# A two-block MLP kernel on one core: one padded round trip through DRAM per tile, and a re-ordered switch between its two phases

## What is computed

```python
# block 0
agg_w, agg_b = per_batch_mix(att(cond_128))          # att: softmax over 8 experts
h0   = einsum('boi,bih->boh', agg_w, x) + agg_b      # mixes the 64 rows of each batch
main = h0 @ weight.T                                 # 1024 x 1024
w    = top-2 gate of h0, with a capacity count over all 4096 rows
lora = sum_e (w_e * (h0 @ lora_A[e])) @ lora_B[e] / 16
x1   = x + main + lora
# block 1
c1   = grouped_conv1d(x1, 64 -> 64 channels, 4 groups, 9 taps) + ctx + bias
res  = c1 @ W.T + b
w1   = softmax_e(<c1 Wq_e, c1 Wk_e>)
out  = x1 + res + sum_e w1_e * (c1 @ A[e]) @ Bm[e]
```

## Time and profile before

| | |
|---|---|
| median of three runs | 1290.04 us (1289.51 to 1290.76) |
| the profiled execution | 1290.04 us |
| its span on the core | 1288.3 us |
| PE busy | 1279.4 us of the span |
| granted TensorE clock | 1.00 over the span |
| DVE, ACT, POOL busy | 714.7, 280.4, 239.1 us |
| DMA | 141.55 MB, mean 110 GB/s |

### The profile page before, as it was taken

How to read it: one execution, slowest core, us unless ns; L and a number is a source line. 1 busy time by engine, 2 the same in 40 slices (tenths; PEclk the granted TensorE clock), 3 DMA queues, 4 the chain that set the end, 5 groups by cost and what they waited for, 6 DMA issues and landing times.

```text
span 1288.3 us, 20752 instructions
## 1 busy us (share of the span) xinstructions
PE 1279.4 (99%) x7223; PEld 1193.6 (93%) x7223; DVE 714.7 (55%) x1727; ACT 280.4 (22%) x515; POOL 239.1 (19%) x173
## 2 busy tenths in 40 slices
PE   9999999999999999999999999999999999999998
PEld 8999999999999998989889889988988988988997
DVE  6887877767777776634434444444443444344432
ACT  6323322222322234211111111111111111111110
POOL 2344522232322330001001001001100100100100
PEclk9999999999999999999999999999999999999999
DMA  8245433333333357434223323322422322342310
GB/s 292 91 133 182 147 114 109 120 128 114 118 109 112 104 195 236 121 88 119 72 71 115 91 69 104 104 69 88 119 70 84 113 80 69 106 102 70 91 47 33
DMA packets 83735, 141.55 MB, mean 110 GB/s; under 512 B 6641, under 2 KB 52081, under 8 KB 83697
## 3 DMA queue, kind: packets, MB, share of 16 engines
q1 hardware_dynamic: 83696, 141.06, 36.1%
HBM read 88.59 MB, written 52.45 MB: 109 GB/s over the span
## 4 chain that ended last, share of the span: by engine, by line
PE 92%; DVE 4%; DMA 1%; issue 1%; POOL 0%; ACT 0%; SPq 0%; DVEq 0%; POOLq 0%; ACTq 0%
PE ps L1205 28%; PE ps L1207 27%; PE ps L1206 27%; PE ps L1346 6%; PE ps L1347 2%; DMA staging<-in_w 1%; DMA z<-in_cpack 0%; DVE weights L877 0%; DVE row L910 0%; POOL mixw L581 0%; DVE part L902 0%; DVE mix_hl L887 0%; PE ps L1439 0%; DVE mixs L884 0%; PE ps L1322 0%
## 5 line engine op out<-in xcount | busy, mean ns | idle before, releaser
L1205 PE MATMUL ps<-weights,lhs_h 128*128 128x512 f32 (+2 forms) x1408 | 498.4, 354 | 0.8 <-issue 0.8
L1207 PE MATMUL ps<-weights,lhs_l 128*128 128x512 f32 (+2 forms) x1408 | 490.2, 348 | 0.0
L1206 PE MATMUL ps<-weights,lhs_h 128*128 128x512 f32 (+2 forms) x1408 | 489.1, 347 | 0.0
L1205 PEld LDWEIGHTS ps<-weights,lhs_h 128*128 128x128 f32 x1408 | 264.8, 188 | 23.9 <-issue 1.1
L1207 PEld LDWEIGHTS ps<-weights,lhs_l 128*128 128x128 f32 x1408 | 264.3, 188 | 20.8
L1206 PEld LDWEIGHTS ps<-weights,lhs_h 128*128 128x128 f32 x1408 | 264.7, 188 | 20.1
L645 POOL TENSOR_TENSOR xo<-row,wsum 128x512 f32<-128x512 f32 x60 | 76.8, 1306 | 662.4 <-DMA out_x<-xo 662.4
L1205 PE MATMUL ps<-weights 128*128 128x396 f32 x384 | 133.0, 346 | 0.0
L1206 PE MATMUL ps<-weights 128*128 128x396 f32 x384 | 132.3, 344 | 0.0
L1207 PE MATMUL ps<-weights 128*128 128x396 f32 x384 | 132.2, 344 | 0.0
L1177 DVE TENSOR_TENSOR xo<-ps,xo 128x512 f32<-128x512 f32 x64 | 43.1, 691 | 148.3 <-PE ps L1207 148.2
(11 more groups left out here) (151 smaller groups left out, 1436.0 us busy)
## 6 DMA issues: line engine op xcount, KB each, us to landing
row<-spill SPq DMA_DIRECT2D x30, 576.0 KB, 4.3
xo<-in_xt SPq DMA_DIRECT2D x32, 512.0 KB, 3.8
z<-x_round SPq DMA_DIRECT2D x64, 256.0 KB, 5.3
out_x<-xo SPq DMA_DIRECT2D x31, 512.0 KB, 2.7
x_round<-row SPq DMA_DIRECT2D x60, 256.0 KB, 2.0
row<-in_xr SPq DMA_DIRECT2D x31, 394.0 KB, 3.2
spill<-row SPq DMA_DIRECT2D x31, 394.0 KB, 4.0
staging<-in_w SPq DMA_DIRECT2D x8, 832.0 KB, 6.6
```

The lines of the kernel that those rows point to most:

```text
L1205: pe.matmul(out_ap, lhs[0], rhs[0], start=first, stop=False, skip_group_check=True)
L1206: pe.matmul(out_ap, lhs[0], rhs[1], start=False, stop=False, skip_group_check=True)
L1207: return pe.matmul(out_ap, lhs[1], rhs[0], start=False, stop=last, skip_group_check=True)
```

## The change

It has five parts.

1. x1_round is laid out as rows of 129 elements, one for each batch and position group, with the zero column in place. Each store writes four pieces of 512 B per partition instead of one of 2 KB; one z_load reads whole rows of 516 B on all 128 partitions instead of two that read 512 B on 64 partitions. Both stores of a buffer count on one semaphore, and z_load waits once. The order of positions on the partitions, and with it the convolution's weights, is laid out anew.
2. The POOL memset of z moves from tile 2 to tile 6, and at the end of tile 6 SP waits for it and writes z to both buffers of x1_round (padded); the first x1_store waits for these two.
3. The four chunks split aside move from tiles 4 to 7 to tiles 1 to 4. N1+4 is now split by POOL in the first tile of phase B, not by DVE.
4. At tile 24, DVE's x_low goes ahead of the second route; before, it came after the next y_low and evict.
5. At the switch the orders of SP, ACT, DVE and PE change: loads of N1+3, N1+5 and N1+6 go out earlier, z_high(0) and z_low(0) come after the splits of N1+3, N1+6 is split ahead of gates(2) and of z(1), and PE has no second(0,0,2,0,4) between n=5 and n=6 any more (it comes after conv(1,0), as in the other tiles).

```diff
-        x1_round = nc.dram_tensor("x1_round", (2, 2, P, D // 2), F32, kind="Internal").ap()
+        x1_round = nc.dram_tensor("x1_round", (2, BG, GC * S, W), F32, kind="Internal").ap()
+        def half_rows(u, h):
+            return x1_round[u].rearrange("b (c s) w -> (b c) s w", s=S)[:, S // 2 * h:S // 2 * h + S // 2, :]
...
-        by_pool = (N_LB0, N_CONV, N_LB1, N1)
+        by_pool = (N_LB0, N_CONV, N_LB1, N1, N1 + 4)
-        aside = {4: N_LB0, 5: N_CONV, 6: N_LB1, 7: N1}
+        aside = {1: N_LB0, 2: N_CONV, 3: N_LB1, 4: N1}
...
-                    sp.dma_start(x1_round[u, h], src[:, q]).then_inc(x1_out[h], 16)
+                    sp.dma_start(half_rows(u, h)[:, :, w:w + P],
+                                 src[:, 512 * h:512 * h + 512].rearrange("p (s i) -> p s i", i=P)
+                                 ).then_inc(x1_out[u], 16)
...
-                for h in range(2):
-                    sp.wait_ge(x1_out[h], out_done)
-                    sp.sem_inc(passed_sp, 1)
-                    w = 1 - h
-                    sp.dma_start(z[64 * h:64 * h + 64, :, w:w + P], positions(u, h)).then_inc(z_in, 16)
+                sp.dma_start(z[:, :, :], x1_round[u].rearrange("b q w -> q b w")).then_inc(z_in, 16)
...
+                if at(t, 6):
+                    sp.wait_ge(blank, 1)
+                    for k in range(2):
+                        sp.dma_start(x1_round[k].rearrange("b q w -> q b w"), z[:, :, :]).then_inc(padded, 16)
...
-            z_load(0, 0)
             chunk(N1 + 3)
+            z_load(0, 0, 0)
             chunk(N1 + 4)
+            x1_store(1, 1)
             sp.wait_ge(mix_read[2], TILES - 2)
             spill12(TILES - 3, 1)
-            x1_store(1, 1)
+            chunk(N1 + 5)
             sp.wait_ge(mix_read[2], TILES - 1)
             spill12(TILES - 2, 0)
-            chunk(N1 + 5)
-            z_load(1, 1)
+            z_load(1, 1, 0)
+            chunk(N1 + 6)
...
-                if at(t, 2):
+                if at(t, 6):
                     pool.memset(z[:, :, :], 0.0).then_inc(blank, 1)
...
+                if at(t, 0):
+                    split_lo(N1 + 4)
...
+            split_hi(N1 + 3)
+            y_high(TILES - 2, 2)
             z_high(0)
-            y_high(TILES - 2, 2)
-            split_hi(N1 + 3)
             split_hi(N1 + 4)
             conv_high(0, 0)
             y_high(TILES - 1, 2)
             split_hi(N1 + 5)
+            split_hi(N1 + 6)
             z_high(1)
-            split_hi(N1 + 6)
...
-                    if at(t, CATCH_UP + 1):
-                        y_low(t + 2, 0)
-                        evict(t - 1, 1 - u, 2)
-                        x_low(t + XB - 1, (b + XB - 1) % XB)
-                    else:
-                        evict(t - 1, 1 - u, 2)
-                        y_low(t + 2, 0)
+                    evict(t - 1, 1 - u, 2)
+                    y_low(t + 2, 0)
...
+                    if before_end(t, XB):
+                        x_low(t + XB, b)
                     if at(t, CATCH_UP):
                         route(t + 2, u)
-                    elif before_end(t, XB):
-                        x_low(t + XB, b)
...
             y_low(T1, 2)
+            x1_add(1, 1)
+            evict(T1, 1, 2)
+            split_lo(N1 + 3)
+            y_low(T2, 2)
             z_low(0)
-            y_low(T2, 2)
-            evict(T1, 1, 2)
-            x1_add(1, 1)
-            split_lo(N1 + 3)
             evict(T2, 0, 2)
             conv_read_low(0, 0, 0)
             y_low(T3, 2)
-            split_lo(N1 + 4)
             evict(T3, 1, 2)
             split_lo(N1 + 5)
+            split_lo(N1 + 6)
             gates(2, 0, 1)
...
-            main(T3, B3, 2, 0, 2)
+            main(T3, B3, 2, 0, 3)
+            mix(T2, B2, 2)
             pe.wait_ge(*low_of(N_CONV))
             conv(0, 0)
-            mix(T2, B2, 2)
             conv(0, 1)
-            main(T3, B3, 2, 2, 8)
+            main(T3, B3, 2, 3, 8)
...
-                        if n == 6:
-                            second(0, 0, 2, 0, 4)
```

More of the change, by code:

```diff
@@ L86, in program @@
         cond_rows = nc.dram_tensor("cond_rows", (B, C), F32, kind="Internal").ap()
-        x1_round = nc.dram_tensor("x1_round", (2, 2, P, D // 2), F32, kind="Internal").ap()
+        x1_round = nc.dram_tensor("x1_round", (2, BG, GC * S, W), F32, kind="Internal").ap()
         def f32(ap):
             return ap.bitcast(F32)
-        def positions(u, h):
-            return x1_round[u, h].rearrange("(b c) (s i) -> (c s) b i", c=GC, i=P)
+        def half_rows(u, h):
+            return x1_round[u].rearrange("b (c s) w -> (b c) s w", s=S)[:, S // 2 * h:S // 2 * h + S // 2, :]
         weights = sb("weights", [P, J * OUT1 * 2], F32R)
@@ L224, in program @@
         x1_out, z_in = pair("x1_out"), sem("z_in")
-        blank = sem("blank")
+        blank, padded = sem("blank"), sem("padded")
         z_hi, z_lo = sem("z_hi"), sem("z_lo")
@@ L432, in x1_store @@
                 src = x1_row(t, u)
+                if at(t, 0):
+                    sp.wait_ge(padded, 32)
                 if later(t, 2):
-                    loaded_before, = counts(t * 32 - 32)
+                    loaded_before, = counts(t * 16 - 16)
                     sp.wait_ge(z_in, loaded_before)
@@ L438, in x1_store, with z_load @@
                     sp.wait_ge(x1_ready, ready[h])
-                    q = slice(512 * h, 512 * h + 512)
-                    sp.dma_start(x1_round[u, h], src[:, q]).then_inc(x1_out[h], 16)
[L442 to L445, removed]
+                    w = 1 - h
+                    sp.dma_start(half_rows(u, h)[:, :, w:w + P],
+                                 src[:, 512 * h:512 * h + 512].rearrange("p (s i) -> p s i", i=P)
+                                 ).then_inc(x1_out[u], 16)
+            def z_load(t, u, it):
+                out_done, split_before = counts((it + 1) * 32, t * 2)
+                sp.wait_ge(x1_out[u], out_done)
                 if later(t, 1):
@@ L448, in z_load @@
                     sp.wait_ge(z_lo, split_before)
-                    sp.sem_inc(passed_sp, 1)
-                for h in range(2):
-                    sp.wait_ge(x1_out[h], out_done)
-                    sp.sem_inc(passed_sp, 1)
-                    w = 1 - h
-                    sp.dma_start(z[64 * h:64 * h + 64, :, w:w + P], positions(u, h)).then_inc(z_in, 16)
+                sp.sem_inc(passed_sp, 1)
+                sp.dma_start(z[:, :, :], x1_round[u].rearrange("b q w -> q b w")).then_inc(z_in, 16)
             def phase_a(t, b, it):
@@ L522, in _ @@
             spill12(TILES - 1, 1)
-            chunk(N1 + 6)
             chunk(N1 + 7)
@@ L526, in _, with next_row @@
             sp.wait_ge(spilled0[1], TILES // 2 * 16)
-            def next_row(t, u):
-                added, left = counts(t * 2 - 2, t * 16 - 16)
+            def next_row(t, u, it):
+                added, left = counts(t * 2 - 2, it * 32)
                 sp.wait_ge(xb_ready, added)
-                for h in range(2):
-                    sp.wait_ge(x1_out[h], left)
-                    sp.sem_inc(passed_sp, 1)
+                sp.wait_ge(x1_out[u], left)
+                sp.sem_inc(passed_sp, 1)
                 load_row(t, u)
@@ L547, in phase_b @@
                 if before_end(t, 3):
-                    next_row(t + 3, 1 - u)
+                    next_row(t + 3, 1 - u, it + u + 1)
                 if before_end(t, 2):
-                    z_load(t + 2, u)
+                    z_load(t + 2, u, it + 1)
                 if at(t, TILES - 1):
@@ L786, in z_high @@
                     if h == 0:
-                        act.wait_ge(z_in, t * 32 + 32)
+                        act.wait_ge(z_in, t * 16 + 16)
                         if later(t, 2):
@@ L1073, in conv_read_low @@
                 if at(t, 0):
-                    for k in range(2):
-                        dve.wait_ge(x1_out[k], 16)
+                    dve.wait_ge(x1_out[0], 32)
                     dve.wait_ge(xb_ready, 2)
@@ L1183, in phase_b @@
                     z_low(1)
-                    split_lo(N1 + 6)
                     split_lo(N1 + 7)
@@ L1433, in phase_b @@
                     pe.wait_ge(y_read, t * 2)
-                    second(t, u, 2, 0, 4)
+                second(t, u, 2, 0, 4)
                 if nxt:
@@ L1501, in laid_out @@
                     band[:, s, m, :, r, :] = w[:, :, :, tap].transpose(2, 0, 1)
-    a["conv"] = band.reshape(GC, 2, S // 2, -1).transpose(1, 0, 2, 3).reshape(P, 2 * GRP * P)
+    a["conv"] = band.reshape(P, 2 * GRP * P)
     return {k: np.ascontiguousarray(w) for k, w in a.items()}
```

## The result

| kernel | median us (range, runs) | before beside it | ratio, 95% interval |
|---|---|---|---|
| changed | 1299.53 (1296.63 to 1301.11, 4) | 1290.22 | 1.0069 [1.0051, 1.0089] |
| changed, a second time | 1299.03 (1296.95 to 1300.45, 4) | 1290.52 | 1.0068 [1.0052, 1.0084] |

A forecast was written before the change was run, and what follows sets the result against it. PE, busy 1279.4 of 1288.3 us, was taken as the bound. Terms 2.4 (tile 2) + 0 + 1.2 (tile 24) + 0.4 (switch) + 0 gave +4.0 on 1290.04: 1294.0 us, 8-in-10 range 1289.8 to 1298.

The forecast's parts named there:

- the term for z(0) in part 5: At the switch, z arrives at about 489, just in time for conv(0,0): 0.3 us, bounds 0 and 2.5.
- a sign of being wrong: In phase B, the stores landing beyond 6 us after issue would show the prediction wrong.
- The term beside it: At the switch, POOL's next add can hold gates(2) for one half, 1.3 us; taken as 0.5 us.
- The 2 us that the prediction gave this rule: In phase B, pieces not starting at 256 B multiples shift z by about 2 us, inside the cover; cost 0.
- Tile 2: POOL's early split holds DVE's line 890 until 73.6, fully exposed on PE: +2.4 us, bounds 0 and 2.8.
- The zeros: Writing zeros at tile 6's end makes later row loads some 5 us late: 0, up to 2 us if pieces are slow.
- Tile 24: x_low and evict ahead of y_low(27,0) add 1.6 us, less hold by POOL's add: +1.2 us, bounds 0.8 to 1.6.
- The switch's orders: At the switch, old gaps close but PE waits 1.7 us at tw_turn(2): -0.4 us before the added terms.
- Phase B: In the rest of phase B, later z is covered by idle time: cost 0, period of 24.6 us unchanged.
- Rival B: Small pieces are slow: conv(0,0) waits 2.5 us at the switch, zeros cost 2; +8, 1298 us; chance 0.12.

## Why the prediction was wrong

**The step that failed** is the term for z(0) in part 5: "a store to 512 B pieces lands between 2.0 us (the 2 KB stores now) and 5.3 us (the loads of 512 B pieces) after its issue ... I take 0.3 for it, bounds 0 and 2.5". Its upper bound came from loads. The stores took 7.1 and 10.5 us at the switch, beyond the 6 us that the prediction itself had named as a sign of being wrong, and z came at 497.3 instead of 489. The runs with aligned pieces show why: for the most part it is where a stored piece begins.

The step also looked only at z. The stores slow the transfers that share the queue with them, and SP stands behind them with the loads of N1+4 and then N1+6. That chain ended at tw_turn(2), and the slow load of N1+3 at mix(T2,2). By the ratios the whole change costs 4.1 us with aligned stores and 8.8 with these: the term of 0.3 was about 4.6 (2 to 7), its bound of 2.5 most likely too low. The term beside it, 0.5 for POOL's add holding gates(2), measured 1.1 in this profile (1.35 us instead of 0.29) and 0 in the second, where gates(2) began 0.09 us before POOL's add.

The prediction weighed a page's rule on pieces that don't start at a multiple of 256 B (the Trainium skill, DMA: Bandwidth & Descriptors, section How a descriptor splits into AXI transactions). It speaks of what a transaction can read; here the loads of 516 B pieces did not suffer, and the stores did. The 2 us that the prediction gave this rule, hidden in phase B, were worked out from no row, and it did not ask what the rule would do at the switch.

**The clock was not in the sum.** After gaps of 2 to 3 us PE ran at 1.2 GHz for some microseconds: 1.6 us lost behind tile 2, 1.6 in conv(0) and 1.4 behind tw_turn(2) in the first profile (from the spacing of the matmuls), 1.5 in all in the second. Over all runs of the changed kernel the granted clock was 0.996 to 0.999, of the kernel before 0.999 or 1.

**Tile 2: the mechanism right, the size too small.** Line 890, now 895, was predicted to last 2.8 us and lasted 3.33; PE was to wait until about 82.0 and waited until 82.24. The gaps grew by 3.0 us in the first profile, 2.4 or 2.5 in the second and with the splits alone, against +2.4. But with the small gaps of tiles 3 and 5 the splits alone cost 3.5 us, and in the first profile the lower clock came on top. The Trainium skill's rule on the port pair (SBUF — State Buffer, section SBUF: two separate sides) is borne out once more: 0.47 us became 2.60 to 3.33 beside POOL's split, while instructions that read PSUM went on: in the run with the round trip alone, lines 908 and 916 took their usual 0.57 and 0.56 us beside POOL's split of 3.79 us.

**The zeros: right with these splits, for a reason I had not seen.** In the changed kernel tile 8 has no gap. With the splits in tiles 4 to 7 it would have 1.4 to 2.8 us. I gave 0 to 2. That the term of 0 came out is luck: it hung on part 3.

**Tile 24: the mechanism right, the size half.** PE's gap went from 0.7 to 1.2 us, +0.5 instead of +1.2 (1.0 to 1.6 us over the five profiles with that part). POOL's next add held the second route for 0.1 us only, where the working left 0.4; the rest was not traced.

**The switch's orders: right in sum.** Taken alone they change nothing (0.9998 [0.9988, 1.0008]), where the working has -0.4, and +0.5 for POOL's add. Two errors met in it: N1+6 landed in 5.2 us instead of 6.6, and POOL's add held gates(2) for 1.1 us instead of 0.5. In the changed kernel the gap at lora_first(2) closed and that at the start of phase B fell from 0.9 to 0.5 us, as predicted; tw_turn(2) took their place.

**Phase B: right.** The period is full, though each store lands 3.5 us later.

**The account.** The splits alone cost 3.5 us, the orders alone nothing, tile 24 0.5. That leaves 4.5 to 5.3 of the 8.5 to 9.3 us measured, and making the stores aligned takes 4.6 off (2 to 7). The parts do not add up strictly, since the zeros and the splits share a cost: the round trip alone cost 6.4. Rival B, small pieces that are slow, named the right term and its sign, but not all of the places: the zeros cost nothing in the changed kernel, and at the switch the loss came through the loads of weights. That alignment and not size makes the pieces slow, no row of the kernel before could show.

## What to carry to other kernels

When a layout change makes rows of 516 B out of 512, price the stores apart from the loads, and by where each piece begins. Whether this kernel could have both, aligned pieces and one load with the zero column in place, is not shown: the run with aligned pieces computes something else, since the zero column puts half of the pieces one element into their rows. The old round trip with its 2 KB pieces came out at the same time (ratio 1.0035 against 1.0032) and leaves nothing out, so the single load bought nothing. Where the DMA queue is the busiest at a switch, a slow transfer is paid by everything issued behind it and by the in-order program that waits for it, so follow the chain of the loads, not only the data that the transfer carries. And a new gap of 2 to 3 us in a full PE can cost more than its length, here up to 1.6 us more.

## What the runs showed of the hardware

- Stores of 256 KB in 512 pieces of 512 B: 2.6 to 2.9 us when each starts at a multiple of 256 B, 4.6 with 4 B of shift, 5.5 at a pitch of 516 B. Loads from the same layouts (256 or 516 KB each): 4.4 to 4.8, 4.0 and 3.8 us. Why the store and not the load is slow stays open.
- In 20 us at the switch, where these stores run beside weight loads, the queue carried 212 GB/s at a share of 0.93, with aligned stores 313 at 0.95.
- Behind idle times of PE of about 2 to 3 us the granted clock sometimes fell to 1.2 GHz and sometimes not. It fell behind 1.76 (changed kernel with late splits), 1.90 (shifted pieces), 2.21, 2.88 and 3.03 us (changed kernel) and 2.34 us (the same, second profile); it did not behind 1.93 and 2.40 us in that second profile, nor behind 2.67 us with the round trip alone.
- A DVE instruction with two SBUF inputs that began after an add or a split of POOL was held by it: 0.47 us became 2.60 to 3.33, and gates(2) 0.29 us became 1.35 to 1.37 in five profiles. In the sixth it began 0.09 us before POOL's add and took 0.28.
